# A fused two-layer graph kernel, second step: the second hop starts one product later, GpSimd's row norms stand ahead of its bracket, and the last product runs in two parts

## The reference, cut to what matters

```python
R = S + eye(N); R = R / R.sum(-1)          # rows normed
Xf = Xa = X
for n in range(2):
    A = top_p_attention(Xa, W1, W2, W3)    # softmax, keep 0.9 of each row's mass, renorm
    Xf = R @ Xf
    Xa = A @ Xa
    Z = Z + Xf @ U1[n].T + Xa @ U2[n].T
out = layernorm(x + layernorm(X + Z))
```

## Time and profile before

| | us |
|---|---|
| three runs, median | 3933.82 |
| lowest and highest | 3932.32 to 3934.52 |
| the profiled execution, own time | 3931.79 |
| its span, first to last instruction | 3930.0 |
| mean granted TensorE clock | 0.981 |

### The profile page before, as it was taken

How to read it: one execution, slowest core, us unless ns; L and a number is a source line. 1 busy time by engine, 2 the same in 40 slices (tenths; PEclk the granted TensorE clock), 3 DMA queues, 4 the chain that set the end, 5 groups by cost and what they waited for, 6 DMA issues and landing times.

```text
span 3930.0 us, 66291 instructions
## 1 busy us (share of the span) xinstructions
PE 3600.7 (92%) x25368; PEld 3036.9 (77%) x25368; DVE 3582.6 (91%) x6269; ACT 3069.0 (78%) x3107; POOL 1312.3 (33%) x1467
## 2 busy tenths in 40 slices
PE   8888888888888869999999989999999999999995
PEld 5777777777777747778777768888888788888884
DVE  4999999999999969999999499999999799999996
ACT  6999999999999965555555378888888788888871
POOL 0000000000000000111111155555655469999995
PEclk9999999999999989999999999999999999999997
DMA  3112112112112140000000323333333433333331
GB/s 110 49 56 84 56 56 84 56 56 80 59 56 72 68 132 14 21 17 17 17 21 19 105 89 95 98 98 99 99 102 104 148 107 109 115 116 116 115 120 45
DMA packets 155581, 302.71 MB, mean 77 GB/s; under 512 B 16634, under 2 KB 116986, under 8 KB 151010
## 3 DMA queue, kind: packets, MB, share of 16 engines
q1 hardware_dynamic: 155234, 298.22, 23.7%
HBM read 256.54 MB, written 41.62 MB: 76 GB/s over the span
## 4 chain that ended last, share of the span: by engine, by line
DVE 55%; PE 20%; ACT 14%; POOL 6%; issue 4%; DVEq 0%; DMA 0%; SPq 0%; ACTq 0%; POOLq 0%; PEldq 0%; PEld 0%
DVE b L1370 13%; DVE b L1368 13%; PE ps L898 8%; PE ps L971 6%; DVE b L1421 5%; ACT b L1217 4%; ACT b L1218 4%; DVE b L1588 4%; DVE b L1366 3%; DVE b L1479 3%; DVE b L1477 3%; DVE b L1458 2%; POOL b L595 2%; PE ps L957 2%; POOL b L592 2%
## 5 line engine op out<-in xcount | busy, mean ns | idle before, releaser
L898 PE MATMUL ps<-b 128*128 128x257 f32 x4096 | 911.5, 382 | 20.5 <-DMA b<-in_adjTb 11.5
L971 PE MATMUL ps<-b 128*128 128x257 f32 x4096 | 903.2, 380 | 0.0
L898 PEld LDWEIGHTS ps<-b 128*128 128x128 f32 x4096 | 776.8, 190 | 146.1 <-issue 18.4
L971 PEld LDWEIGHTS ps<-b 128*128 128x128 f32 x4096 | 772.2, 190 | 113.4 <-ACT b L1155 0.8
L832 PE MATMUL ps<-cb,b 128*128 128x128 f32 x4096 | 507.1, 280 | 199.6 <-ACT b L1045 161.0
L832 PEld LDWEIGHTS ps<-cb,b 128*128 128x128 f32 x4096 | 456.7, 144 | 248.7 <-ACT b L1045 183.9
L1368 DVE SCALAR_TENSOR_TENSOR b<-b 128x4096 f32<-128x4096 f32 x128 | 566.5, 4425 | 12.4 <-ACT b L1039 8.2
L1370 DVE CUSTOM_DVE_ANT_0 b<-b 128x4096 f32<-128x4096 f32 x128 | 566.4, 4425 | 4.4
L558 POOL TENSOR_TENSOR cb<-cb 128x1 f32<-128x1 f32 x32 | 39.5, 1233 | 1392.4 <-DVE cb L1350 1392.4
L1052 ACT ACTIVATE b<-ps 128x1024 f32<-128x1024 f32 x512 | 491.6, 1067 | 9.5 <-PE ps L832 9.3
L1045 ACT ACTIVATE b<-b 128x4096 f32<-128x4096 f32 x128 | 482.6, 3770 | 2.9 <-DVE b L1372 2.5
(11 more groups left out here) (204 smaller groups left out, 4884.8 us busy)
## 6 DMA issues: line engine op xcount, KB each, us to landing
b<-in_adjTb SPq DMA_DIRECT2D x256, 512.0 KB, 3.8
b<-in_adj SPq DMA_DIRECT2D x32, 2048.0 KB, 8.4
h_d<-b SPq DMA_DIRECT2D x63, 128.0 KB, 1.8
b<-h_d SPq DMA_DIRECT2D x63, 128.0 KB, 2.6
b<-in_xT SPq DMA_DIRECT2D x4, 1024.0 KB, 8.5
b<-in_xT SPq DMA_DIRECT2D x32, 128.0 KB, 8.1
gx_d<-b SPq DMA_DIRECT2D x32, 128.0 KB, 1.8
X_d<-b SPq DMA_DIRECT2D x32, 128.0 KB, 8.2
```

What stands on the lines that cost most here:

```text
L898: last = mm(b[:, 0:XA], aj[:, q % AJR, e, :], xf[:, j, :], start=(j == 0), stop=(j == NT - 1))
L971: last = mm(o[:, 0:XA], at[:, q % ATR, b, :], xa[:, j, :], start=(j == 0), stop=(j == NT - 1))
```

## The change

`pairs_in` becomes `rows_in`, which gives single products: up to stage 14 the same as before (2n+2 and 2n+3), stage 15 product 32 alone, stage n from 16 to 30 products 2n+1 and 2n+2, stage 31 product 63. In stage 31 that product is cut in 24 and 8 column tiles with `gather_level` between; in stage 15 `gather_level` stands behind product 32. On GpSimd the first row of a stage is normed ahead of that stage's bracket, the second where both were; the bracket of stage 14 takes the second row of stage 14 in its middle, behind the operation that releases ScalarE. The final slots (`fslot`) of pairs 0 to 13 move one stage later, so that pair 13 sits in slot 31. On SP the loads at the head of the step are in another order, and in stage 0 the store of the first rows goes behind all loads of that stage.

```diff
-    fslot = {min(max(HT + m - RLEAD + 2, 2 * m + 4), NT + 1): m for m in range(HT)}
+    fslot = {min(max(HT + m + 2, 2 * m + 4), NT + 1): m for m in range(HT)}
-    def pairs_in(n):
...
+    def rows_in(n):
+        if n < HT - 1:
+            return [2 * n + 2, 2 * n + 3]
+        return [r for r in (2 * n + 1, 2 * n + 2) if NT <= r < 2 * NT]
...
-            for q in range(NQ):
-                reload(q)
             sp.wait_ge(g["ks"], 16 * NT)
             sp.wait_ge(s_bar, 5 * kS[0])
...
-            ld(u2, U2T[1].rearrange("(k p) n -> p k n", p=128), s_l1)
...
+            for c in range(NCH):
+                adjchunk(AJR + c)
+                for q in range(NQ // NCH * c, NQ // NCH * (c + 1)):
+                    reload(q)
             gxload(0)
-            adjpairs(-1, 0)
+            ld(u2, U2T[1].rearrange("(k p) n -> p k n", p=128), s_l1)
             sp.wait_ge(g["xp"], 1)
             qload(1, 2)
-            adjpairs(-1, 1)
+            adjrow(-1, 1)
...
-                if HT in pairs_in(n):
+                if n == 0:
+                    adjrow(n, 0)
+                    adjrow(n, 1)
+                    rstore(n - 1)
+                elif n == HT - 1:
                     rstore(n - 1)
                     sp.wait_ge(g["ys"], 16 * NT)
                     sp.wait_ge(g["R"], NT * NCH)
                     chunked(xf, y_d)
-                adjpairs(n, 0)
-                if HT not in pairs_in(n):
+                    adjrow(n, 0)
+                else:
+                    adjrow(n, 0)
                     rstore(n - 1)
-                adjpairs(n, 1)
+                    adjrow(n, 1)
...
                     tt(tst[:, t % 2:t % 2 + 1], a(8), ahalf, ALU.pow).then_inc(g["bt"], 1)
+                    if between is not None:
+                        r_post(between, rows_in(between)[1:])
...
                     if s == 1:
-                        for p in pairs_in(n - 1):
-                            r_post(p)
+                        if n == 0:
+                            r_post(-1, rows_in(-1))
+                        elif n != HT - 1:
+                            r_post(n - 1, rows_in(n - 1)[1:])
...
+                    if s == 1 and n < NT:
+                        r_post(n, rows_in(n)[:1])
                     if s == 1 and n + 2 < NT:
-                        bracket(n + 2)
+                        bracket(n + 2, n if n == HT - 2 else None)
...
                     if s == 1:
-                        for p in pairs_in(n):
-                            Rmul(2 * p)
-                            if n >= 1:
+                        early = 1 <= n < NT and len(rows_in(n)) == 2
+                        if n == NT - 1:
+                            r = 2 * NT - 1
+                            b = Rstart(r)
+                            Rpart(r, b, 0, NT - TBK)
+                            gather_level(n)
+                            Rpart(r, b, NT - TBK, NT)
+                        else:
+                            for r in rows_in(n):
+                                if early and r > rows_in(n)[0]:
+                                    gather_level(n)
+                                Rmul(r)
+                            if n < NT and not early:
                                 gather_level(n)
-                            Rmul(2 * p + 1)
-                        if n == 0 or n == NT - 1:
-                            gather_level(n)
```

More of the change, by code:

```diff
@@ L426, in reload @@
             def reload(q):
[L427 to L428 removed]
+                sp.wait_ge(st[0]["av"], (NT - 1) * NCH + q // 2 + 1)
+                sp.wait_ge(st[0]["acc"], CT * (q + 1))
                 for i in range(2):
[L430 removed]
+                    sp.wait_ge(st[0]["xd"][i], 16 * (CT // 2) * (q + 1))
                 ld(xa[:, CT * q:CT * (q + 1), 0:256],
@@ L483, in gxload, with adjrow @@
                         ld(gxi[:, i, :], tile_of(gx_d, 2 * p + i), g["gi"])
-            def adjpairs(n, half):
-                for p in pairs_in(n):
-                    for q in range((2 * p + half) * NCH, (2 * p + half + 1) * NCH):
+            def adjrow(n, i):
+                for r in rows_in(n)[i:i + 1]:
+                    for q in range(r * NCH, (r + 1) * NCH):
                         adjchunk(q + AJR)
             def rstore(n):
[L491 to L496, removed]
+                for r in rows_in(n):
+                    sp.wait_ge(g["yd"], r + 1)
+                    ld(tile_of(y_d if r < NT else z_d, r % NT), yr[:, r % 2, :], g["ys"])
+                if n < HT - 1:
+                    gxload(n + 2)
+            for c in range(NCH):
+                adjchunk(AJR + c)
+                for q in range(NQ // NCH * c, NQ // NCH * (c + 1)):
+                    reload(q)
             gxload(0)
-            adjpairs(-1, 0)
+            ld(u2, U2T[1].rearrange("(k p) n -> p k n", p=128), s_l1)
             sp.wait_ge(g["xp"], 1)
             qload(1, 2)
-            adjpairs(-1, 1)
+            adjrow(-1, 1)
             for n in range(LAST + 4):
@@ L582, in levels, with bracket @@
                     nc.gpsimd.partition_all_reduce(levr, lev, 128, RMAX).then_inc(g["lr"], 1)
-                def bracket(t):
+                def bracket(t, between=None):
                     a = lambda i: ptm[:, i:i + 1]
@@ L630, in accumulate, with r_post @@
                     tt(hh, pzs, xa[:, t, 0:256] if s == 0 else hin, ALU.add).then_inc(g["acc"], 1)
-                def r_post(p):
-                    for i in range(2):
-                        r = 2 * p + i
+                def r_post(n, rows):
+                    for r in rows:
+                        i = r % 2
                         po.wait_ge(g["rd"], r + 1)
@@ L1300, in _ @@
                     else:
-                        acts(n + 1, [2 * p + i for p in pairs_in(n) for i in range(2)], n)
+                        acts(n + 1, rows_in(n), n)
                 barrier(ac, kS[s])
```

14 lines of the change are left out of this document (4 added, 10 removed).

## The result

| | us |
|---|---|
| before, median of four runs | 3933.07 (3930.98 to 3934.52) |
| changed, median of four runs | 3964.93 (3963.47 to 3966.73) |
| changed / before | 1.0082, 95% interval 1.0070 to 1.0094 |
| span of the changed kernel's profiled execution | 3964.3 (before 3930.0) |

The change makes the kernel 0.8% slower. The page's first line does not show where: the busy times hardly move against the earlier trace rows.

A forecast was written before the change was run, and what follows sets the result against it. TensorE was taken to set the 50.6 us stage, with VectorE (48.2) and the GpSimd-ScalarE loop close. Terms -3.2 + 30.5 - 4.6 + 3.5 + 5.3 = +31.5 on span 3930.0, plus 3.8, gave 3965.3 us; range 3933 to 3988.

The forecast's parts named there:

- (a): Start of the step: tile 0's flag no longer waits for TensorE, -3.2 us.
- (b): Stages 1 to 14: norms delay bracket's end to T+22.0 (T: start of VectorE's first pass), 52.6 us a stage, +30.5.
- (d): Stages 16 to 18: bracket falls behind the fourth pass, 52.0 us a stage against 50.6, +3.5 us.
- (c): Hop change, stage 15: one product fewer, the mask at T+57.4 and next first pass at T+57.7, -4.6 us.
- (e): Stages 19 to 29: a wide gap takes the rest of the bracket, TensorE is the bound again, 0.
- (f): Stages 30 and 31: flag ready as VectorE asks, 0; bound +3.3 us if GpSimd meets the masks.
- (g): Tail: pair 13's final norms behind the last mask delay row 30's statistics and the end, +5.3 us.
- the norms slip through: Rival for stages 1 to 14: GpSimd's requests interleave better, (b) is 0, 3924.5 us; chance 0.18.
- The slow clock: Rival: TensorE's idle in each stretched stage costs 2.5 us at low clock, 3981 us; chance 0.12, shared with more holds.
- Half the loss: Rival: norms and bracket pack into one operation fewer, (b) is +8 to +12, 3945 us; chance 0.10.

The follow-up runs named there:

- experiment 8: norms_back plus product 32 halved round the flag, pair 13's last norm later, tile 29's scaling earlier: 3923.74 us; with product 32 also evicted behind the exponentials: 3922.11 us.
- norms_back: The changed kernel with both row norms of a stage behind the bracket again (stage 14: both in its middle): 3930.32 us, ratio 0.9994.
- Experiment 2, before_ahead: The kernel before with only the first row's norm moved ahead of the bracket: 3962.38 us, ratio 1.0073.
- two_ahead: norms_back with the first two operations of the first row's norm (add, reciprocal) ahead of the bracket: 3940.41 us, ratio 1.0021.

## Why the prediction was right, point by point

Forecast 3965.3, measured 3964.93; the forecast's case came, with its mechanism. That the number is hit within 0.4 us is luck. The profiled span is 3964.3 and not 3961.5, 2.8 more, of which 2.2 are a later start of the second step (see (a)). And the sum fits only because its misses cancel: (b) and (d) came out 7.2 us below the forecast, (a), (c), (e), (f) and (g) 7.7 above.

- *(a) start, forecast -3.2, measured -3.1.* The flag of tile 0 no longer waits. From the first pass of tile 0 to the end of its mask are 67.7 us in all ten kernels with this head, and 70.8 before. In the changed kernel's profile mask 0 ends only 0.9 sooner, because that pass starts 2.2 us later there (2245.25, before 2243.00); it starts between 2241.8 and 2245.3 in the ten kernels, although none of them changes step one.
- *(b) norms ahead of the bracket, forecast +30.5, measured +24.1.* The decisive step, L599 at T+22.0 to T+22.4, was measured at T+22.1, and the four passes are lost as in the walk. Mis-sized was the sum over the stages, 6.4 us too much. I took 14 intervals of 52.6. But the first norm that stands ahead of a bracket stands ahead of tile 2's, so mask 1 can't feel it: the first interval is 48.35 (before 48.3), which is VectorE's own work and 4.2 less than I took. The second is 54.2, where VectorE waits 2.74 for ScalarE and 2.67 for the flag; that gives 1.6 back. The other twelve are 52.3 each, 3.8 less in all. The mean of 50.4 that I worked with had the short interval in it.
- *(c) hop change, forecast -4.6, measured -3.9.* L599 ended at T+22.0, the norm at T+24.7 (3069.04; T is 3044.38), and the product began 5.66 us later. It took 16.8 us, as forecast with the 16.61 of the earlier trace rows, but for another reason. Before, the product ran without a wait at a granted clock of 0.88 (3056 to 3073); here the clock was 1.00 (3075 to 3092), and the last quarter waited 2.38 us for S, although I had written that the loads' cover is not lost. The mask ended at T+57.0, 0.4 sooner than forecast. The 0.7 that are missing are in how I counted: I took the interval from first pass to first pass, and T lies 1.45 us behind mask 14, not 0.3, since VectorE waits for ScalarE. Not in my list was that ScalarE's step sizes come from behind the norm in the bracket: hidden in the changed kernel with one row there, 5.07 us with two (experiment 8).
- *(d) stages 16 to 18, forecast +3.5, measured +2.7.* This is the loss against the kernel before. norms_back, without the norms ahead, gains 2.3 here, so against it the norms cost 5.0.
- *(e) stages 19 to 29, forecast 0, measured +4.3: the step that failed.* L599 ends at T+16.8, near the T+17.2 that I said. But I held TensorE's 50.6 against VectorE's 48.2, which I had read in stages 15 and 0, ahead of the final statistics. These add two operations, 1.41 and 0.38 us (L1450 and L1454 in the changed kernel). So VectorE had no slack there even before the change: in the first hop its flag waits 2.2 us for TensorE, from the stage of tile 22 on it waits for next to nothing (0.15 us once). What the norm ahead of the bracket holds VectorE for is therefore lost. In the late stages shown and beside them these holds are 0.23 on the mask and 0.17 on the second pass (4.71 and 4.66 against 4.48 and 4.49), and one of 0.43 on a small operation (L1538, 0.71 in this stage and 0.28 in others). With them VectorE's work comes to 50.8; measured are 50.9. TensorE's transposes start 4.2 us behind mask 20 and 1.6 behind mask 29: it catches up, VectorE is the bound. Experiment 2 shows 3.9 us from the norm alone.
- *(f) stages 30 and 31, forecast 0, measured +0.9 in all,* inside its bound. norms_back shows the case I had bounded at +3.3, GpSimd meeting the masks, with +4.2 in 30 to 31.
- *(g) tail, forecast +5.3, bounds 4 and 6, measured +6.9.* The two norms and the wait of VectorE are there as forecast. norms_back has +5.5 and before_ahead +1.0, so most of the 1.4 above norms_back goes with the norms ahead; which step carries it I did not find.

The rivals: *the norms slip through* falls by the GpSimd rows; what it forecast for a kernel without the loss, 3924.5, was 3930.3 in norms_back: the hop change and the three stages behind it gave 7.2 us there and not 11.4, and intervals 29 to 31 cost 3.4 that it had at nothing. *The slow clock* falls by the granted clock of 1.00 over masks 0 to 14, with 20 us of idle in them. The Trainium skill (page "TensorE: Matmul & The Clock Gate", section "Part 1: The HAM clock gate") lets the clock follow how busy the engine has been; that agrees. *Half the loss* did not come either; it is what two_ahead shows, with masks 51.2 apart and 3940.4 us.

The Trainium skill's rule (page "SBUF — State Buffer", section "SBUF: two separate sides"), that VectorE with two SBUF operands and GpSimd exclude one another for a whole instruction, agrees with GpSimd's side in every row here where a pass was running: 3.5 to 4.8 us for operations that take 0.2 to 0.75 alone. On VectorE's side the holds were 0.2 to 0.5 us, less than the 0.73 of the GpSimd operation beside them.

## What to carry to other kernels

Where VectorE runs long passes with two operands back to back, count GpSimd's work ahead of a release in gaps, not in microseconds: what fits in the gap is free (one operation cost nothing), what does not costs GpSimd a whole pass (5.1 us with two operations ahead). The stage then grows only by what goes beyond the slack of the loop behind the release, here 4.6 us: by 0.6 us with two operations, 1.7 with four. If the delay moves the asker past the next start, it stays in every later stage. Read an engine's own work in each kind of stage, with everything that only late stages do, before calling another one the bound. A gain at one join (here 6.5 us) is kept only as far as the next loop allows (0.9 in the profiled executions, 2.4 in the medians, which they can't tell from nothing).

## What the runs showed of the hardware

The cost of a small GpSimd operation depends on the moment at which it asks: 4.65 us at T+0.4 for 257 columns, 0.74 in the gap for the 256 of L648. Under a pass a one-column operation costs as much: L641 took 4.61 in the late stage and 0.55 in a gap. And it is steady: in the thirteen stages behind the first, L599 ended 22.0 to 22.1 us behind the first pass's start, so that a walk through the gaps gave a stage's interval within 0.3 us. The loss also keeps itself up: a late bracket makes the stage's products and levels late, and so the next norm asks just behind the start of a pass.
